# A recommender tower on one core: groups of three features, a ring of gathers, pair products in portions, and a feature-major embedding copy that TensorE reads at a stride

## What is computed

```python
e = jnp.stack([tbl_0[ids[:, 0]], ..., tbl_26[ids[:, 26]]], axis=1)      # 2048 x 27 x 128
interactions = jnp.einsum('bfd,bgd->bfg', e, e)
z = jnp.concatenate([e.reshape(B, -1), interactions[:, _TRIU_I, _TRIU_J]], axis=1)
h = jnp.concatenate([z, dense_ctx], axis=1)                             # 3823 columns
h = jnp.maximum(h @ W_top1 + b_top1, 0.0)                               # 512
h = jnp.maximum(h @ W_top2 + b_top2, 0.0)                               # 256
y = h @ W_top3                                                          # 1
```

## Time and profile before

| | |
|---|---|
| median of 3 runs | 590.26 us (589.81 to 592.77) |
| span of the profiled execution | 769.5 us |
| TensorE (PE) busy | 537.4 us, 70% of the span |
| TensorE weight load (PEld) busy | 434.5 us, 56% |
| GpSimd (POOL) busy | 415.9 us, 54% |
| ScalarE (ACT) busy | 246.5 us, 32% |
| VectorE (DVE) busy | 154.0 us, 20% |
| DMA | 51.10 MB, mean 66 GB/s |
| granted TensorE clock, mean | 0.856 of full |

### The profile page before, as it was taken

How to read it: one execution, slowest core, us unless ns; L and a number is a source line. 1 busy time by engine, 2 the same in 40 slices (tenths; PEclk the granted TensorE clock), 3 DMA queues, 4 the chain that set the end, 5 groups by cost and what they waited for, 6 DMA issues and landing times.

```text
span 769.5 us, 15280 instructions
## 1 busy us (share of the span) xinstructions
PE 537.4 (70%) x6224; PEld 434.5 (56%) x6224; DVE 154.0 (20%) x269; ACT 246.5 (32%) x370; POOL 415.9 (54%) x441
## 2 busy tenths in 40 slices
PE   3406856767578677876776787658778767677884
PEld 2304645656456555755555675546667555566773
DVE  3304211112021111211111221211111121121222
ACT  3414422233132233323233332332323233232441
POOL 6766463663646546564664656466465646556110
PEclk9858777999879798889899898987889898988997
DMA  6515311412414123241422424131332424133110
GB/s 208 172 49 179 96 45 43 73 49 67 51 61 56 47 72 42 75 52 35 84 49 75 45 78 51 59 58 47 76 45 77 52 67 47 48 77 46 56 41 7
DMA packets 52704, 51.10 MB, mean 66 GB/s; under 512 B 36652, under 2 KB 39897, under 8 KB 52680
## 3 DMA queue, kind: packets, MB, share of 16 engines
q0 software_dynamic: 13984, 28.42, 20.4%
q1 hardware_dynamic: 38696, 22.34, 9.9%
HBM read 40.22 MB, written 10.49 MB: 66 GB/s over the span
## 4 chain that ended last, share of the span: by engine, by line
PE 47%; another core or an unknown queue 20%; issue 19%; ACT 7%; DVE 2%; DMA 2%; SPq 1%; ACTq 0%; DVEq 0%
PE p_hid L572 12%; PE p_hid L573 11%; PE p_hid L574 11%; PE p_prod L637 7%; ACT emb L341 5%; PE p_quad L567 5%; DVE emb_low L446 2%; ACT emb_high L338 1%; PE p_hid_t L603 1%; DMA w_stage<-w_dense_dram 1%; ACT w_high L330 1%; SPq L226 0%; DMA pairs_dram<-prod 0%; DMA inter<-pairs_dram 0%
## 5 line engine op out<-in xcount | busy, mean ns | idle before, releaser
L301 POOL DMA_INDIRECT gathered<-tbl_dram,idx x432 | 412.5, 955 | 301.9 <-issue 125.0
L572 PE MATMUL p_hid<-w_high,emb_high 128*128 128x512 f32 x432 | 204.5, 473 | 156.1 <-DVE emb_low L446 95.4
L572 PEld LDWEIGHTS p_hid<-w_high,emb_high 128*128 128x128 f32 x432 | 95.5, 221 | 182.9 <-DVE emb_low L446 100.5
L573 PE MATMUL p_hid<-w_low,emb_high 128*128 128x512 f32 x432 | 190.6, 441 | 0.0
L338 ACT ACTIVATE emb_high<-p_quad 128x512 fp32r<-128x512 f32 (+1 forms) x111 | 66.3, 597 | 386.9 <-remote 183.6
L574 PE MATMUL p_hid<-w_high,emb_low 128*128 128x512 f32 x432 | 190.2, 440 | 0.0
L446 DVE TENSOR_TENSOR emb_low<-p_quad,emb_high 128x512 fp32r<-128x512 f32 (+1 forms) x112 | 75.2, 671 | 431.9 <-ACT emb L341 230.9
L341 ACT ACTIVATE emb<-p_quad 128x512 f32<-128x512 f32 (+1 forms) x111 | 128.9, 1161 | 0.0
L574 PEld LDWEIGHTS p_hid<-w_high,emb_low 128*128 128x128 f32 x432 | 94.4, 218 | 23.7
L573 PEld LDWEIGHTS p_hid<-w_low,emb_high 128*128 128x128 f32 x432 | 95.8, 222 | 18.0
L637 PE MATMUL p_prod<-emb 128*27 128x27 f32 x4096 | 53.6, 203 | 47.6 <-issue 47.0
(11 more groups left out here) (40 smaller groups left out, 237.6 us busy)
## 6 DMA issues: line engine op xcount, KB each, us to landing
w_stage<-w_dense_dram SPq DMA_DIRECT2D x27, 256.0 KB
gathered<-tbl_dram,idx POOLq DMA_INDIRECT x432
pairs_dram<-prod SPq DMA_DIRECT2D x16, 432.0 KB
pairs_dram<-prod SPq DMA_DIRECT2D x16, 208.0 KB
inter<-pairs_dram SPq DMA_DIRECT2D x187, 14.6 KB
w_stage<-w_dram SPq DMA_DIRECT2D x2, 256.0 KB
idx<-ids_dram SPq DMA_DIRECT2D x16, 13.5 KB
w_stage<-w_pairs_dram SPq DMA_DIRECT2D x1, 256.0 KB
```

Of the source, the lines that this page charges most:

```text
L301: pool.indirect_dma_start(gathered[:, f, :], None, tables[f], bass.IndirectOffsetOnAxis(ap=idx[:, par, f:f + 1], axis=0),).then_inc(quad_g ...
L572: nc.tensor.matmul(dst, high, w_high, start=start, stop=False)
L573: nc.tensor.matmul(dst, high, w_low, start=False, stop=False)
```

## The change

The kernel is written anew around five points.

- **Groups of three features** (`FEATS`, nine `GROUPS`) replace the quads. TensorE transposes a group two groups ahead of its layer 1, instead of one quad.
- **A ring** of six groups (`RING`, 18 features) replaces the buffer of 27 features. GpSimd's gathers for a group wait until the group six before it is transposed. `emb_high` and `emb_low` become rings of three groups (`SPLIT`).
- **Portions**: the 128 pair products are cut into eight calls of 16. Three run after the last group of the tile, three after the first group of the next, two after its second group. `emb` becomes two buffers for that. In the last tile they run in one piece.
- **The layout of `emb`** is feature-major, `[P, NF, P]`. ScalarE writes it densely; both operands of a pair product are `emb[par][:, :, sample]`, 27 numbers 128 apart, 512 bytes from one to the next.
- Around them: six staging buffers for weights instead of four; all ids of tiles 1 to 15 in one load; the ids' and the identity's loads waited for apart; ScalarE, VectorE, GpSimd and SyncE with all tiles written out, without loops. Layer 2 and layer 3 of a tile come one tile later than before.

The gathers themselves, 432 of 128 rows, and the three passes of each layer are the same.

```diff
-    QUADS = [list(range(f, min(f + 4, NF))) for f in range(0, NF, 4)]
-    NQ = len(QUADS)
+    FEATS = 3
+    GROUPS = NF // FEATS
+    RING = 6
+    SPLIT = 3
...
-    STAGES = 4
+    STAGES = 6
+    CALLS = 8
+    PER_CALL = ROWS_Q // CALLS
...
-        idx = sb("idx", [P, 2, NF], I32)
-        gathered = sb("gathered", [P, NF, D])
-        emb = sb("emb", [P, P, NF])
-        emb_high = sb("emb_high", [P, NF, P], F32R)
-        emb_low = sb("emb_low", [P, NF, P], F32R)
+        idx = sb("idx", [P, TILES, NF], I32)
+        gathered = sb("gathered", [P, RING, FEATS, D])
+        emb = [sb(f"emb_{k}", [P, NF, P]) for k in range(2)]
+        emb_high = sb("emb_high", [P, SPLIT, FEATS, P], F32R)
+        emb_low = sb("emb_low", [P, SPLIT, FEATS, P], F32R)
...
+            for t in range(TILES):
+                if t == 1:
+                    pool.wait_ge(ids_loaded[1], 16)
+                for g in range(GROUPS):
+                    slot = ring_slot(t, g)
+                    wait(pool, group_transposed, t * GROUPS + g - RING + 1)
+                    for k in range(FEATS):
+                        f = g * FEATS + k
+                        pool.indirect_dma_start(
+                            gathered[:, slot, k, :], None, tables[f],
+                            bass.IndirectOffsetOnAxis(ap=idx[:, t, f:f + 1], axis=0),
+                        ).then_inc(group_gathered[slot], 16)
...
-                nc.scalar.activation(emb[:, :, f0:f0 + n].rearrange("p b f -> p f b"), bank,
-                                     ACT.Copy).then_inc(quad_copied, 1)
+                nc.scalar.activation(emb[t % 2][:, f0:f0 + FEATS, :],
+                                     bank_of(t, g), ACT.Copy).then_inc(group_copied, 1)
...
-            def pair_products(t, first):
+            def pair_products(t, par, calls):
...
-                            x = emb[:, s * GROUPS + b * BATCH_G + k, :]
+                            x = emb[par][:, :, s * ROWS_Q + b * BATCH_G + k]
...
+            def tile(t, par, depth=2):
...
                 other = (par + 1) % 2
+                for g in range(GROUPS):
+                    if g < GROUPS - 2:
+                        transpose_group(t, g + 2, par)
+                    else:
+                        transpose_group(t + 1, g + 2 - GROUPS, other)
+                    layer1_group(t, g, par, depth == 0)
+                    if g == 0 and depth >= 1:
+                        pair_products(t - 1, other, [3, 4, 5])
+                    if g == 1 and depth >= 1:
+                        pair_products(t - 1, other, [6, 7])
+                    if g == 2 and depth >= 2:
+                        layer2(t - 2)
+                    if g == GROUPS - 2 and depth >= 1:
+                        layer1_pairs(t - 1, other)
+                    if g == GROUPS - 1:
+                        pair_products(t, par, [0, 1, 2])
+                        if depth >= 1:
+                            transpose_hid1(t - 1)
...
             def last_tile(t, par):
+                other = (par + 1) % 2
+                for g in range(GROUPS - 1):
+                    if g < GROUPS - 3:
+                        transpose_group(t, g + 2, par)
+                    layer1_group(t, g, par)
...
+                    if g == GROUPS - 3:
+                        transpose_group(t, GROUPS - 1, par)
+                pair_products(t, par, range(CALLS))
+                layer1_pairs(t - 1, other)
+                layer1_group(t, GROUPS - 1, par)
                 transpose_hid1(t - 1)
```

More of the change, by code:

```diff
@@ L125, in dlrm_tower @@
         p_hid1 = [pb(f"p_hid1_{k}", [P, HID1]) for k in range(2)]
-        p_quad = [pb(f"p_quad_{k}", [P, 4, P]) for k in range(2)]
+        p_group = [pb(f"p_group_{k}", [P, 4, P]) for k in range(2)]
         p_prod = [pb(f"p_prod_{k}", [P, 512]) for k in range(2)]
@@ new lines, in copy_whole, with group_copies @@
+            def copy_whole(t, g):
+                if g == 0:
+                    wait(act, prod_bank_done, (t - 1) * NB)
+                f0 = g * FEATS
+                nc.scalar.activation(emb[t % 2][:, f0:f0 + FEATS, :],
+                                     bank_of(t, g), ACT.Copy).then_inc(group_copied, 1)
+            def group_copies(t, g):
+                if t == 0:
+                    for n in range(FEATS * g, FEATS * (g + 1)):
+                        weight_high(n)
+                act.wait_ge(group_transposed, t * GROUPS + g + 1)
+                if t == LAST and g == GROUPS - 1:
+                    copy_whole(t, g)
+                    copy_high(t, g)
+                else:
+                    copy_high(t, g)
+                    copy_whole(t, g)
+                if t == 0 and g == GROUPS - 1:
+                    for n in range(NF, len(STAGED)):
+                        weight_high(n)
@@ L540, in _ @@
             dve.wait_ge(zeroed, 1)
-            dve.wait_ge(consts_loaded, CONSTS * 16)
-            tile(0, 0, first=True)
-            tile(1, 1, second=True)
-            for t in range(2, 5):
-                tile(t, t % 2)
-            with dve.Fori(0, TILES // 2 - 3) as i:
-                for k in range(2):
-                    tile(2 * i + 5 + k, (1 + k) % 2)
-            tile(TILES - 1, (TILES - 1) % 2, final=True)
-            last = TILES - 1
-            last_inter_to_low(last, [0])
@@ L552, in _ @@
-            layer3(last - 1, (last - 1) % 2)
-            last_inter_to_low(last, [1, 2])
-            last_copy_hid1(last, last % 2)
-            last_hid1_split(last)
-            layer3(last, last % 2)
+            group_low(0, 0)
+            group_low(0, 1)
+            for t in range(TILES):
+                for g in range(GROUPS):
+                    ahead = t * GROUPS + g + 2
+                    if ahead < TILES * GROUPS:
+                        group_low(ahead // GROUPS, ahead % GROUPS)
+                    if g == 0 and t == 0:
+                        dve.wait_ge(consts_loaded, CONSTS * 16)
+                    if g == 1 and t >= 2:
+                        hid1_to_low(t - 2)
+                    if g == 2 and t >= 1:
+                        copy_products(t - 1)
+                    if g == 4 and t >= 2:
+                        layer3(t - 2)
+                    if g == GROUPS - 2 and 1 <= t < LAST:
+                        inter_to_low(t - 1)
+                        copy_hid1(t - 1)
@@ L570, in three_passes, with landings @@
+            def landings(t, g, par):
+                first = (par * GROUPS + g) // RING + 1
+                return first + (t - par) * GROUPS // RING if isinstance(t, int) else first + (t - par) // 2 * 3
             def three_passes(dst, high, low, w_high, w_low, start, stop):
@@ L622, in layer2 @@
                 last.then_inc(hid2_done, 1)
-            def pair_products(t, first):
-                pe.wait_ge(quad_copied, (t + 1) * NQ)
-                if first:
-                    pe.wait_ge(zeroed, 1)
-                for b in range(NB):
-                    if b == 0:
+            def pair_products(t, par, calls):
+                for n in calls:
+                    if n == 0:
+                        pe.wait_ge(group_copied, (t + 1) * GROUPS)
                         wait(pe, prod_copied_act, t)
-                    else:
+                    if n == CALLS // NB:
@@ L638, in pair_products @@
                                                     x, x, start=True, stop=True)
[L639 to L641 removed]
+                    if n % (CALLS // NB) == CALLS // NB - 1:
+                        last.then_inc(prod_bank_done, 1)
+            def tile(t, par, depth=2):
                 other = (par + 1) % 2
[L644 to L658 removed]
```

374 lines of the change are left out of this document (150 added, 224 removed).

## The result

The changed kernel takes 691.84 us (684.70 to 692.94, four runs) where the kernel before takes 590.54 (589.81 to 592.77, four runs): ratio 1.169, 95% interval 1.163 to 1.175. The forecast was 591.8 us with a range of 558 to 632, so the measured time lies 60 us above the range and 100 above the forecast. For the experiments one thing must be known: in some sessions every kernel, the one before too, takes longer in all of its runs (the kernel before 772 to 775 us in the median, the changed one 820) and its recorded execution has the pauses of the earlier trace rows, so the sessions are called undisturbed (kernel before at 590 to 592) and paused, and a run is compared with others of its own kind of session alone.

A forecast was written before the change was run, and what follows sets the result against it. The prediction took GpSimd's rate of issuing gathers as the bound, with TensorE's costs hidden behind it. Only the end added: 590.26 + 0.8 + 0.7 = 591.8 us, range 558 to 632.

The forecast's parts named there:

- TensorE's tile, 30.8 us: TensorE's work per changed tile: 20.7 + 2.7 + 0.5 + 1.5 + 5.4 us, still under the gathers' 33.7.
- belonging to the recorded execution: Remote waits in the 769.5 us trace: read as absent from the 590.26 us runs, about 179 us.
- Bound by the gathers, 581.8 of 590: Whole kernel before: GpSimd's 432 gathers at 1.25 us plus start, landing and end sum to 581.8 us.
- the 8.5 us: Part of the median run time left over by the gathers' total, unplaced and kept the same on both sides.
- Rival 2: Gathers quicker in runs than in trace, TensorE's chain binds: change faster, 556 or 498 us; chance 0.20.
- Dense copy 0, ring 0: ScalarE's dense embedding copies and GpSimd's lead of 18 features instead of 27: each forecast to cost 0 us.
- I take twice the present cost, 5.4 us.: Strided read in TensorE's pair products: 5.4 us per tile against 2.7; upper bounds 28, or 7 with overlap.
- rival 1: Strided read makes TensorE the bound once a tile's products exceed 8.3 us: slower, 630 to about 870 us; chance 0.18.
- Cost 0 to 1 us per tile: Later store and reload of pair products: 37 us chain against 10 groups, 37.5 us; TensorE's cost covered by the ring.
- The end, +0.8 and +0.7 us: Exposed tail: nine products before the last pair products add 0.8 us, doubled stride work 0.7 (0 to +5).
- Slower had 0.34: Chance of a slower changed kernel: 0.12 from the forecast's own range, 0.18 and 0.04 from two rivals.
- rival 3: Ring too short for real pauses: one or two GpSimd stops of 5 us, 600 us; chance 0.04.

The follow-up runs named there:

- e17: The kernel before, unchanged, run again in an undisturbed session to get a recorded execution without pauses: 589.75 us.
- e16: Changed kernel with dense read (row-major copy) and all pair products in one piece after their own tile's ninth group, undisturbed: 590.44 us, ratio 0.999 to the kernel before.
- e15: Changed kernel with dense read of the pair products' copy and 29 dummy products ahead of TensorE's first transposes, undisturbed: 601.93 us, ratio 1.014 to the kernel before.
- e18: Changed kernel with 29 dummy products (116 instructions) ahead of TensorE's first transposes, undisturbed: 639.95 us, ratio 1.085 to the kernel before.
- e3: Changed kernel with TensorE's loop over pairs of tiles written out as straight code, paused session: 788.76 us, ratio 1.020 to the kernel before.
- e11: Kernel before with 12 products of 512 columns per tile replacing its 128 short pair products, paused session: 723.92 us, ratio 0.934 to the kernel before.
- e10_before_shift: Kernel before with 42 dummy products ahead of TensorE's first transposes and a wait for zeroing their PSUM bank, paused session: 769.89 us, ratio 0.997.
- e14: Kernel before with 30 products of 512 columns per tile replacing its 128 short pair products, paused session: 782.14 us, ratio 1.008 to the kernel before.

## Why the prediction was wrong

The step that failed is the one that put TensorE's tile, 30.8 us, under the 33.7 us of the gathers and called all of TensorE's costs hidden. The tile takes 37.6 us, and 8.3 more after each of five jumps back, for which the sum had no term. The gathers themselves were as forecast. Step by step:

- **The pauses "belonging to the recorded execution".** Right for the runs it was held against: e17 spans 587.9 us without any. Wrong as a rule: in four sessions all runs were long, and every recorded one had them.
- **Bound by the gathers, 581.8 of 590.** Right, and the best step of the working: 547.3 us at the last gather against 546.4 by its terms. Of the 8.5 us that it could not place, most lie behind the last gather: the last transposes start at 554.04 instead of some 549, and from there 33.9 us remain, not 32.5; another 2 are between span and time.
- **Rival 2 (quicker gathers).** Wrong: the median gather takes 0.94 to 0.95 us in every recorded execution, paused or not, and e17 issues one per 1.26 us.
- **Dense copy 0, ring 0.** Right: 486 ns; and the 89 us at the ring come from TensorE's pace. With the same ring, e16 waits 3.4.
- **"I take twice the present cost, 5.4 us."** Mis-sized: 7.0 as rows, 6.8 net, so 27 ns per recorded product where the forecast took 21 (dense, they take 13 in e15). It is at the lower of the two upper bounds (7). By the sum this alone would be harmless: 20.7 + 2.7 + 0.5 + 1.5 + 7.0 = 32.4 us is under 33.7, and the threshold of rival 1, 8.3 us of products, was not reached. No undisturbed run has it alone; beside the other costs it was worth 38 us (e18 to e15). The rule of the Trainium skill that stood beside it (Advanced Engine Details and Errata, section SBUF Cachelines) has the right sign, 27 ns against 13, and no size.
- **"Cost 0 to 1 us per tile" for the later store and reload.** This failed. The chain of 37 us was set against 10 groups at the gathers' pace, but for TensorE, once it falls behind, a group takes 2.42 us and not 3.75, so it comes to the pairs early: it waits 2.85 us and pays 1.55 more for nine products at the low clock. These waits are covered only as long as the gathers are slower, and here the stride had used up that cover. With the dense read these waits and the portions cost 11 us together, in the end (e15 to e16).
- **The sum of TensorE's tile, 30.8 us.** With the products 1.4 more, the wait 2.85, the clock 1.55 and the nine groups 1.0 longer in all (22.4 us against 21.3), it is 37.6, as measured. These are costs that were each looked at alone, and called hidden by the same 2.9 us of slack.
- **No term at all for TensorE's code.** The largest part, 52 us, was in none of the sums or rivals. The rows of the kernel before could not show it, but its page had a hint, queue q8: 18 blocks of 16 KB, where e3, with the loop written out, needs 49 for 12,448 recorded products and weight loads. So the loop was being kept, and a change could lose that.
- **The end, +0.8 and +0.7 us.** Measured +17 from the last gather on. The last transposes start 19.2 us after the last gather (651.54 less 632.3), against 6.7 in e17, since TensorE enters the end behind the gathers; from there 38.7 us remain, against 33.9.
- **Sign and chances.** Slower had 0.34, but by mechanisms that did not act in the form described: the stride of rival 1 took part below its threshold, on top of costs that rival 1 had at nothing, and the ring of rival 3 was not too short.

## What to carry to other kernels

Set every cost that you call hidden against one common slack: add all of them on the engine first, and compare once. When an engine changes from waiting to being waited for, chains through other engines have to be measured by its own pace, no longer by that of the old bound. Before moving code of a long hardware loop, compare the instruction fetches of both kernels; here a loop that no longer stayed cost 52 us, more than the other parts, and 116 recorded instructions ahead of it brought it back.

## What the hardware showed that was not expected

- **TensorE's loop back.** With the body not held, a jump back costs 3.5 to 4.2 and 1.7 to 2.3 us of idle time, and nine products at the low clock, 8.3 us in all where it was worked out. An edit of 116 instructions before the loop decides it (63 blocks and 19, 52 us here). Where it was held, q8 brought no block from 165 to 540 us of e18, which is the loop from its second iteration on.
- **Strided reads.** A weight load and product of 27 elements that step 512 bytes take 26 to 27 ns per recorded product in four column strips, 13 in a dense read (10 in the burst of the earlier trace rows).
- **The pauses.** In paused sessions they return, 22 to 27 times a run before ScalarE's copy in the kernel before, also when no short products run (25 times in e11). During one, TensorE gets its short products about 0.7 us apart while GpSimd goes on; the 42 dummy products of e10_before_shift, with nothing to wait for, show it in the first tile:

```profile
8.73 2.39 PE L692 MATMUL p_prod<-identity 128*27 128x27 f32 x47 [8.73 <-DMA w_rows<-w_dram]
...
13.65 0.20 PE L692 MATMUL p_prod<-identity 128*27 128x27 f32 x1 [0.46 <-issue]
...
14.36 0.20 PE L692 MATMUL p_prod<-identity 128*27 128x27 f32 x1 [0.50 <-issue]
```

  The same chip showed both kinds of session (the runs e11 to e14, kernel before at 775, and e17 and e18, at 591), so they are not a property of one chip. What they are stays open. The Trainium skill (NOTIFIC — the notification-queue block, section Overflow: three behaviours, one of which stalls the engine) describes a setting in which a producer of trace records is stalled while the ring for them is full; no run here shows whether it is that.
